# The first layer's attention output reaches its channels' rows by transfers, and GpSimd divides it there, in place of two turns on the matrix engine

## The reference, cut to what matters

```python
q = _apply_rope(q, sin, cos)
k = _apply_rope(k, sin, cos)
scores = jnp.einsum('bqhd,bkhd->bhqk', q, k) * DH ** (-0.5)
attn = jax.nn.softmax(scores, axis=-1)
o = jnp.einsum('bhqk,bkhd->bqhd', attn, v).reshape(b, s, c)
return o @ w_out + residual
```

## Time and profile before

| | |
|---|---|
| median of 3 runs | 515.12 us (514.9 to 515.36) |
| the profiled execution | 515.57 us, of which span 513.8 us |
| PE busy | 504.3 us, 98% |
| DVE busy | 412.0 us, 80% |
| ACT busy | 344.6 us, 67% |
| POOL busy | 220.4 us, 43% |
| transfers | 45.26 MB, mean 88 GB/s |
| granted PE clock | 0.99 of full speed over the span |

### The profile page before, as it was taken

The page is one execution under the profiler, slowest core; times in us unless marked ns, Lnnn a source line. Parts: engine busy times, 40 slices in busy tenths (PEclk is TensorE's granted clock), DMA queues, the critical chain, the costliest instruction groups (busy, mean ns, idle before and its releaser), DMA issues.

```text
span 513.8 us, 9864 instructions
## 1 busy us (share of the span) xinstructions
PE 504.3 (98%) x3346; PEld 195.1 (38%) x3346; DVE 412.0 (80%) x1059; ACT 344.6 (67%) x677; POOL 220.4 (43%) x253
## 2 busy tenths in 40 slices
PE   9999899999999999999999999999999999999987
PEld 5563423333443244333433334332433333332234
DVE  4876897998897688966898688967899999999226
ACT  1453367776767675777768576777778778777961
POOL 3039749999143420832226430643672045005401
PEclk8899999999999999999999999999999999999999
DMA  6983232242214133110331133210331112211011
GB/s 240 349 273 102 80 93 79 64 143 83 76 53 125 41 124 125 41 43 17 113 122 43 43 97 110 68 49 11 124 124 43 43 43 87 81 44 43 2 41 42
DMA packets 43034, 45.26 MB, mean 88 GB/s; under 512 B 4436, under 2 KB 41572, under 8 KB 42600
## 3 DMA queue, kind: packets, MB, share of 16 engines
q1 hardware_dynamic: 42696, 42.79, 26.6%
q10 hardware_dynamic: 288, 1.84, 0.9%
HBM read 25.46 MB, written 18.87 MB: 86 GB/s over the span
## 4 chain that ended last, share of the span: by engine, by line
PE 75%; DVE 11%; issue 2%; POOL 2%; ACT 2%; POOLq 0%; DVEq 0%; ACTq 0%
PE bank L549 19%; PE bank L532 12%; PE bank L523 10%; PE bank L595 9%; PE bank L512 9%; DVE masked L862 7%; PE bank L623 4%; PE bank L606 4%; PE bank L564 2%; PE bank L584 2%; ACT probs L715 1%; DVE row_max L865 1%; PE bank L557 1%; PE bank L631 1%; POOL XN L836 1%
## 5 line engine op out<-in xcount | busy, mean ns | idle before, releaser
L715 ACT ACTIVATE probs<-bank 128x512 f32<-128x512 f32 x512 | 272.4, 600 | 82.0 <-PE bank L523 81.2
L865 DVE TENSOR_REDUCE row_max<-bank 128x1 f32<-128x512 f32 x256 | 162.9, 684 | 29.5 <-PE bank L532 27.9
L532 PE MATMUL bank<-k_s,q_s 64*128 64x512 f16 x512 | 182.7, 382 | 1.8 <-DVE row_max L865 1.2
L862 DVE CUSTOM_DVE_ANT_0 masked<-bank,mask_bias 128x512 bf16<-128x512 f32 x256 | 162.9, 687 | 13.0 <-PE bank L532 12.0
L512 PE MATMUL bank<-q_s,k_s 64*128 64x512 f16 x512 | 151.8, 381 | 0.9 <-ACT v_aug L783 0.5
L523 PE MATMUL bank<-shift,kx 64*128 64x512 f16 x512 | 148.6, 376 | 0.0
L549 PE MATMUL bank<-probs,v_aug 128*17 128x512 f32 x1024 | 135.4, 598 | 0.7 <-ACT probs L715 0.7
L532 PEld LDWEIGHTS bank<-k_s,q_s 64*128 64x128 f16 x512 | 46.1, 93 | 151.8 <-DVE row_max L862 67.1
L595 PE MATMUL bank<-xT,wqkv 128*128 128x512 f32 x128 | 61.7, 612 | 0.4 <-ACT xT L746 0.3
L523 PEld LDWEIGHTS bank<-shift,kx 64*128 64x128 f16 x512 | 46.8, 95 | 32.0
L512 PEld LDWEIGHTS bank<-q_s,k_s 64*128 64x128 f16 x512 | 31.6, 94 | 13.4 <-ACT probs L715 8.0
(11 more groups left out here) (111 smaller groups left out, 512.3 us busy)
## 6 DMA issues: line engine op xcount, KB each, us to landing
q_parts<-parts SPq DMA_DIRECT2D x64, 128.0 KB
k_parts<-parts SPq DMA_DIRECT2D x64, 128.0 KB
q_s<-q_parts SPq DMA_DIRECT2D x32, 256.0 KB, 2.7
k_s<-k_parts SPq DMA_DIRECT2D x32, 256.0 KB, 3.0
X<-in_x SPq DMA_DIRECT2D x4, 512.0 KB, 7.3
y<-X SPq DMA_DIRECT2D x7, 256.0 KB, 2.2
wc<-in_w_cond ACTq DMA_DIRECT2D x1, 1024.0 KB, 5.1
tables<-in_tables SPq DMA_DIRECT2D x4, 256.0 KB, 7.1
```

Source lines behind the costliest of these rows:

```text
L532: nc.tensor.matmul(bank, m.q_s[slot][rows, i, queries], m.k_s[slot][rows, i, :], start=True, stop=True).then_inc(q.d_made, 1)
L715: act.activation(m.probs[k][:, h, :], bank, ACT.Exp, scale=1.0 if s >= B * NG else float(DH) ** -0.5)\
L862: dve.tensor_tensor_reduce(m.masked[D["max", n, k, h] % ND][:, :], bank, m.mask_bias[:, b, :], 1.0, LOWEST, ALU.add, ALU.max, to)\
L865: dve.tensor_reduce(to, bank, AX.X, ALU.max).then_inc(q.d_done, 1)
```

## The change

For the first layer's 16 groups PE's transposes of oT (L564), DVE's writing of O (L889), PE's turns f0 (L584 from O) and ACT's copies of them (L749) are gone. Instead SP sends oT of group s, once ACT has copied it, with five transfers: the four rows of sums to a tile of 128 x 16 (`sums`), and each head's 16 channels to the partitions of their channels in the buffer O, read as channels by tokens (`raw`). DVE takes the reciprocals of `sums` at the place where L887 stood. SP sends them to DRAM (`inverses_out`) and from there to 64 partitions, each head's row 16 times (`inverses_in`). GpSimd multiplies (`divide`), two instructions of 128 x 512 to a batch, into xT. The second layer is as before.

```diff
-    PIECES[_s] = (turn("f0", _b), (), *one(y(0, _b)))
+    PIECES[_s] = ((), (), *one(y(0, _b)))
...
-        if op == "output" and k == 2 and s:
+        if op == "output" and k == 2 and s > LAYER:
             yield op, s - 1
+        if op == "output" and k == 2 and 0 < s <= LAYER:
+            yield "sums", s - 1
...
+def group_out(s):
+    return 16 * (G + 1) * (s + 1)
+def chunk_rows(g):
+    return slice(G * DH * (g % 2), G * DH * (g % 2 + 1))
+def normalised(b, c):
+    return CT * b + c + 1
...
+        m.raw = [t[:, :, :].rearrange("p t c -> p (t c)").rearrange("p (k n) -> p k n", k=CT) for t in m.O]
+        m.inverse = [m.roped[0][1], m.roped[1][1]]
+        m.sums = sb("sums", [P, KT * G])
+        m.inv_dram = nc.dram_tensor("inverses", [B * NG, G, S], F32, kind="Internal").ap()
@@ tensor: tokens_out @@
-                pe.wait_ge(q.a_done, turned(USES[use]))
+                pe.wait_ge(q.divided, normalised(b, CT - 1))
@@ scalar: copy_output @@
+        elif s:
+            act.wait_ge(q.output_out, group_out(s - 1))
@@ vector @@
+    def invert(s):
+        dve.wait_ge(q.output_out, group_out(s))
+        if s:
+            dve.wait_ge(q.inv_out, 16 * s)
+        dve.reciprocal(m.inv_sum[:, :, :, :].rearrange("p t h w -> p (t h w)"), m.sums[:, :]).then_inc(q.inv_made, 1)
@@ gpsimd @@
+    def divide(b, c):
+        use = USES.index(("f0", b))
+        pool.wait_ge(q.output_out, group_out(NG * b + 2 * c + 1))
+        pool.wait_ge(q.inv_in[c], 32 * (b + 1))
+        await_read(pool, q, use - 2)
+        pool.tensor_tensor(m.xT[use % 2][:, c, :], m.raw[b % 2][:, c, :], m.inverse[c][:, :], ALU.mult)\
+            .then_inc(q.divided, 1)
@@ gpsimd: in the loop over rope(b, i), behind rope(b, i) @@
+            if b == B - 1 and i % 2:
+                divide(0, i // 2)
@@ gpsimd: project(b), behind normal("p1", b) and behind the four splits @@
+        if b < LAST:
+            divide(b + 1, 0)
...
+        if b < LAST:
+            divide(b + 1, 1)
@@ sync @@
+    def raw_output(s):
+        b, g = divmod(s, NG)
+        sp.wait_ge(q.acc_copied, s + 1)
+        if b >= 2:
+            sp.wait_ge(q.divided, normalised(b - 2, g // 2))
+        if s:
+            sp.wait_ge(q.inv_made, s)
+        sp.dma_start(m.sums[:, :], m.oT[DH::W32, :].rearrange("h (c n) -> h c n", n=KT * G)).then_inc(q.output_out, 16)
+        first = chunk_rows(g).start
+        for h in range(G):
+            sp.dma_start(m.raw[b % 2][first + DH * h:first + DH * (h + 1), g // 2, :],
+                         m.oT[W32 * h:W32 * h + DH, :]).then_inc(q.output_out, 16)
+    def inverses_out(s):
+        sp.wait_ge(q.inv_made, s + 1)
+        sp.dma_start(m.inv_dram[s].rearrange("h (c n) -> (h c) n", n=KT * G),
+                     m.inv_sum[:, :, :, :].rearrange("p t h w -> p (t h w)")).then_inc(q.inv_out, 16)
+    def inverses_in(s):
+        b, g = divmod(s, NG)
+        sp.wait_ge(q.inv_out, 16 * (s + 1))
+        sp.wait_ge(q.part_dve, 4)
+        if g % 2 == 0 and b:
+            sp.wait_ge(q.divided, normalised(b - 1, g // 2))
+        sp.dma_start(m.inverse[g // 2][chunk_rows(g), :], m.inv_dram[s].unsqueeze(1).broadcast_to([G, DH, S]))\
+            .then_inc(q.inv_in[g // 2], 16)
@@ sync: the loop over s @@
+        if 0 < s <= LAYER:
+            raw_output(s - 1)
         if exists(s + 1):
             shift(s + 1)
         if s >= 0 and exists(s + 3):
             operands(s + 3)
+        if 0 < s <= LAYER:
+            inverses_out(s - 1)
         for pu, i in PARTS_AT.get(s, ()):
             parts(pu, i)
+        if 0 < s <= LAYER:
+            inverses_in(s - 1)
```

More of the change, by code:

```diff
@@ L29 @@
 GROUPS = LAYERS * B * NG
+LAYER = B * NG
 UNIT = 64.0
@@ L390, in build @@
         q.acc_copied = sem("acc_copied")
+        q.output_out = sem("output_out")
+        q.inv_out = sem("inv_out")
+        q.inv_in = [sem(f"inv_in{i}") for i in range(CT)]
+        q.divided = sem("divided")
         q.shift_high = sem("shift_high")
@@ L569, in turn_tokens @@
         bank = d_free(D[piece]) if kind == "f1" else a_free(A[piece])
[L570 to L582, removed]
+        n = NORMAL.index((kind, b))
+        src = m.XN[n % 2]
+        if h == 0 and n == 0:
+            pe.wait_ge(q.ident_made, 4)
+            pe.wait_ge(q.xn0_made, TPB)
+        elif h == 0 and n == len(NORMAL) - 1:
+            pe.wait_ge(q.xn0_made, 2 * TPB)
+        elif h == 0:
+            pe.wait_ge(q.xn_made, TPB * n)
         for t in range(TPB):
@@ L719, in copy_output @@
         act.wait_ge(q.values_done, KT * (s + 1))
-        if s:
+        if s > LAYER:
             act.wait_ge(q.d_made, D["output", s - 1] + 1)
+        elif s:
+            act.wait_ge(q.output_out, group_out(s - 1))
         act.activation(m.oT[:, :], m.ACC, ACT.Copy).then_inc(q.acc_copied, 1)
@@ L747, in tokens @@
                 .then_inc(q.a_done, 1)
-        if kind == "f0":
-            act.activation(to, bank, ACT.Copy).then_inc(q.a_done, 1)
         if kind == "p1":
@@ L880, in write_output @@
         bank = made(D["output", s]).rearrange("p (t h w) -> p t h w", t=KT, h=G)
-        if g == 0 and 2 <= pu < B + 2:
-            dve.wait_ge(q.a_made, turned(("f0", pu - 2)))
+        if s == LAYER:
+            dve.wait_ge(q.inv_out, 16 * LAYER)
+        if g == 0 and pu < B + 2:
+            dve.wait_ge(q.divided, normalised(pu - 2, CT - 1))
         if g == 0 and pu >= B + 2:
             dve.wait_ge(q.xn_made, TPB * NORMAL.index(("f1", pu - 2 - B)))
-        if s:
+        if s > LAYER:
             dve.wait_ge(q.d_done, D["output", s - 1] + 1)
@@ L1064, in vector @@
                 negate(n)
+        if op == "sums":
+            invert(*at)
         if op == "output":
```

## The result

The changed kernel takes 533.88 us (median of 4 runs, 531.01 to 537.0), the kernel before in the same session 515.07 (514.9 to 515.36): a ratio of 1.0361, interval 1.034 to 1.0383. It is 3.6% slower, where 0.8% faster was forecast, and it lies far outside the range. The profiled execution took 531.01 us and is the fastest of the four; its span is 529.2, so 15.4 us more than before are to be explained. The further 3 us between it and the median are in no trace. (A ratio compares undisturbed runs alone, which leaves out two of the ten runs of e9, 521.0 and 521.32, and none of any other kernel.)

The account below looks back on a forecast made before the run. PE was taken to set the pace, with DVE close behind. The terms 2.7 + 4.2 - 0.3 + 0.5 - 2.0 - 1.2 summed to 3.9 us gained, from 515.12 to 511.2 us; the range was 505.5 to 517.7.

Parts of the forecast that it names:

- The gain: On PE, removing f0 (4.1 us) and the transposes (5.6 + 2.4) brings at most 12.1 us.
- f0's tile: Steps 5, 9, 13 and 17: the tile loses 1.02 us, DVE takes back about 0.35; 2.7 us gained in four.
- tiles with a piece: Ten groups with a piece in tile 2 save 0.47 us each, less 0.5 in all: 4.2 us gained.
- the limit of 503.0: The time if all 12.1 us taken from PE count, the most the change can bring.
- the instant of step 3's reciprocal: DVE's maxima in step 3 resume at 114.2 instead of 111.92, 2.3 us late, because SP's queue is full.
- Fifth, y of batches 1 to 3: PE waits 0.8 us for POOL's second product before y; net loss 0.4 us each, 1.2 in all.
- the tripwire: Sign of being wrong: PE waiting over 2 us for POOL before y means the kernel is slower.
- Fourth, step 3: SP's full queue makes step 3's five transfers land late: 2.0 us lost, and steps 2 and 3 win nothing.
- Third, the bare tiles: Steps 6, 10 and 14: DVE's reciprocal comes 0.5 us late; net loss 0.1 us each, 0.3 in all.
- Step 4: Its tile 1 is long, so this step was to win 0.5 us.
- Rival (b): DVE's reciprocal sets the pace; with landing 1.0 us later the kernel is 2.6 us slower, 517.7; chance 0.22.
- its worst case 517.7: The slow end of the range, the time of the rival where DVE's reciprocal sets the pace.

Follow-up runs that it names:

- e9: The changed kernel with the second layer's parts sent one step later and the mask's rows in step 7, nothing else: 517.1 us, ratio 1.0004.
- e7: The changed kernel with SP's order rearranged, the reciprocal waiting for the sums alone, second-layer parts one step later, mask's rows in step 7: 508.41 us, 0.9867.
- e3: The changed kernel with 14 matmuls on an idle tile ahead of the product y of batches 1 to 3, keeping PE busy: 526.56 us, ratio 1.022.

## Why the prediction was wrong

The gain was sized rightly. f0's tile went to 2.47 and its next to 2.82, tiles with a piece from 4.88 to 4.43, and e7, with the waits mostly gone, took 508.4, between the limit of 503.0 and the forecast. The transfers' issue (0.61 each) and the places of the waits were as written; the instant of step 3's reciprocal was too, with two errors of 0.3 us that cancelled. What failed:

- *Fifth, y of batches 1 to 3* is the step that failed most: "landing like q_s in 2.7 ... It waits 0.8 ... net -0.4 each". It waited 3.57, 3.44 and 2.62 us. The queue took what was computed; the landing was 5.63, 5.25 and 4.78 us and not 2.7. I had priced 128 KB, each DRAM row written to 16 partitions, by the load of q_s, and took no account of the parts ahead of it, with which the transfer engines were still about half busy until 198. About 1 us of the miss is there without parts (3.72 in step 10; why, no run shows), and 1.1 to 1.9 go with the parts: in e9, without them, the same three landings took 3.50 to 3.81. Why the parts cost next to nothing in step 6 (4.11) is open. The prediction named the tripwire itself: over 2 us of PE waiting for POOL means slower.
- *The sum had no term for the clock.* It took PE's idle time at its length. Around waits of 3.57 and 3.44 us the clock fell to 0.50, for about 3.5 and 7 us, and they cost 5.2 and 6.1 us with the tile behind; with PE kept busy (e3) the two tiles were 1.6 and 2.4 us shorter. In step 3 an idle 1.70 was followed by a fall too, in this execution. "Net -0.4 each" became -4.8, -5.9 and -2.7: 13.4 us where 1.2 stood.
- *Fourth, step 3*: the reciprocal's instant was right, its price -2.0 was -4.1. In e3's trace, with nearly the same wait and no fall of the clock, the two tiles lost 2.5: so about 1.6 of the miss is the clock and the rest is small.
- *Third, the bare tiles*: landing 1.7 was 2.0 in most steps and 3.1 in steps 10 and 14, and tiles 2 and 3 together took 6.1, 7.3 and 7.3 us where 5.6 had stood: 0.6, 1.7 and 1.7 lost, not 0.1 each. Step 4, put down as a gain of 0.5, lost 0.7 (its tile 3 took 3.81). Rival (b) described this ("at 1.0 us more to landing") but left y as it was.
- The chance of slower was 0.22 and its worst case 517.7. Each term had both ends, but they were ends of a landing, never of a landing behind 1 MB of other transfers and a clock that can fall behind the wait. In steps 9 and 13 the two add.

What stays open: why the heads landed in 3.1 us in steps 10 and 14 (a packet of instruction code lies there in the transfer records, and that is only a guess), why a wait of 1.6 to 1.7 us in step 3 was followed by a fall of the clock in one execution and not in another, and why e9's runs spread over 9 us where e7's lie within 0.8.

## What to carry to other kernels

Taking work from the engine that sets the pace brings only what the slowest new path lets through: write down the new path (copy, issues, way out, way in, product), with every instruction that its in-order queue already holds, and give it a due time with slack, before its parts are priced. Where it is late in front of the matrix engine, price the clock too: here waits of 3.4 to 3.6 us cost 5.2 and 6.1, one of 2.6 cost 2.7. And when such a change loses, look at the queue's order before giving it up: here the later parts and mask rows were worth 16.8 us as the first edit and 4.0 as the last, and the rearranged queue made the change a gain of 1.3%.

## What the runs showed of the hardware

- A transfer of 16 rows of 2 KB from SBUF to SBUF, issued by SyncE, takes 0.61 us to issue (two of 64 took 1.26 and 1.75), and the last of four lands 2.0 us after its issue begins (3.1 in steps 10 and 14). The Trainium skill (DMA: Bandwidth & Descriptors, Anatomy of one DMA) has about 2.0 us as a fixed cost on GpSimd's path; the rows of SyncE's queue agree with the size.
- A fetch of four DRAM rows, each to 16 partitions (64 x 2 KB), releases its reader 3.7 to 4.2 us after its issue in the changed kernel with no parts ahead of it, and right behind 1 MB of writes after 4.8 to 5.6 in three steps and 4.1 in one.
- Around idle times of PE of 3.57 and 3.44 us the granted clock fell to 0.50, once 1.3 us after PE had come back and once inside the wait, for about 3.5 and 7 us. It did not fall after 2.62 us in step 17. After 1.70 us in step 3 it did; after 1.62 us at the same place in e3 it did not.
- Two of VectorE's 128x16 instructions from SBUF to SBUF (L899 and L901, f16 out) stand still until the GpSimd instruction that is running has ended: up to 2.29 us instead of 0.18. The reciprocal of the same size, f32 out, does not. Long GpSimd instructions are best cut in pieces where VectorE's chain is due.
